# Feed-forward stages: the down product two rows behind the up product, deeper buffers between them, and weight splits on GpSimd tied to finished chunks

## What is computed

```python
x = x + 0.5 * L0_ffn(layernorm(x))      # stage ffn0a
x = x + L0_attn(layernorm(x))
x = x + 0.5 * L0_ffn(layernorm(x))      # stage ffn0b
x = x + 0.5 * L1_ffn(layernorm(x))      # stage ffn1a
x = x + L1_attn(layernorm(x))
x = x + 0.5 * L1_ffn(layernorm(x))      # stage ffn1b

def L0_ffn(x):   # "gated": hidden size 768, integer weights, scale 1/127
    h = silu(x @ wg.T) * (x @ wu.T)
    return h @ wd.T
def L1_ffn(x):   # not gated: hidden size 1024, float weights
    h = gelu(x @ w1 + b1)
    return h @ w2 + b2
```

## Time and profile before

| | us |
|---|---|
| median of 3 runs (2221.59 to 2228.74) | 2226.15 |
| the profiled execution | 2221.8 |
| its span | 2218.8 |
| TensorE busy | 2038.5 (92%) |
| VectorE busy | 1635.1 (74%) |
| ScalarE busy | 1360.3 (61%) |
| GpSimd busy | 512.7 (23%) |
| ffn0a, ffn0b, ffn1a, ffn1b: stretches of the span | 34 to 192, 1007 to 1178, 1178 to 1381, 2022 to 2218.8 |

### The profile page before, as it was taken

One profiled execution on the slowest core, in us unless ns is written; L12 is line 12 of the kernel. 1 busy time (PEld: TensorE's weight loads), 2 busy tenths in 40 slices (PEclk: granted clock), 3 DMA queues, 4 the chain that ended last, 5 costly groups with the idle time before them and its releaser, 6 DMA issues. The chain is left out here.

```text
span 2218.8 us, 44693 instructions
## 1 busy us (share of the span) xinstructions
PE 2038.5 (92%) x16837; PEld 1258.3 (57%) x16837; DVE 1635.1 (74%) x2894; ACT 1360.3 (61%) x2620; POOL 512.7 (23%) x570
## 2 busy tenths in 40 slices
PE   3998889999999999987998999959999999989998
PEld 2887733333333333355877888834444444448887
DVE  6776699999999999847774445868888888817333
ACT  3444348888888888833444544716777777753444
POOL 2100142211231231242003111973221212112110
PEclk9999979999999999998998999968999999989999
DMA  4002843253363363131001000785454655320000
GB/s 143 1 0 95 315 68 55 50 78 71 71 101 66 74 98 66 38 91 41 0 0 62 1 0 1 195 252 83 77 100 83 110 99 104 71 57 20 29 19 29
DMA packets 124377, 161.68 MB, mean 73 GB/s; under 512 B 54669, under 2 KB 77901, under 8 KB 124181
## 3 DMA queue, kind: packets, MB, share of 16 engines
q1 hardware_dynamic: 107108, 119.67, 25.9%
q0 software_dynamic: 16256, 37.82, 6.5%
q10 hardware_dynamic: 816, 1.57, 0.2%
HBM read 94.02 MB, written 63.70 MB: 71 GB/s over the span
## 5 line engine op out<-in xcount | busy, mean ns | idle before, releaser
L1523 ACT ACTIVATE att_probs<-att_s_exp 128x512 f32<-128x512 f32 (+3 forms) x1792 | 888.2, 552 | 222.1 <-PE att_s_exp L1422 98.9
L1555 DVE TENSOR_REDUCE att_maxes<-att_s_max 128x2 f32<-128x1024 f32 x640 | 773.6, 1223 | 69.9 <-PE att_s_max L1383 65.5
L1446 PE MATMUL att_o_ps<-att_probs,att_v_st 128*32 128x256 f32 (+1 forms) x6912 | 527.2, 377 | 19.5 <-ACT att_o_sb L1502 18.8
L1446 PEld LDWEIGHTS att_o_ps<-att_probs,att_v_st 128*32 128x32 f32 x6912 | 138.1, 108 | 268.3 <-issue 165.4
L1549 DVE CUSTOM_DVE_ANT_0 att_s_max<-att_s_max,mask_q 128x384 f32<-128x384 f32 (+3 forms) x512 | 237.2, 521 | 28.1 <-PE att_s_max L1383 24.8
L1383 PE MATMUL att_s_max<-first_k,first_q 62*128 62x512 f32 (+3 forms) x672 | 153.4, 444 | 41.3 <-DVE att_neg_max L1534 24.0
L1422 PE MATMUL att_s_exp<-first_q,first_k 64*128 64x512 f32 (+3 forms) x672 | 175.4, 476 | 2.6 <-ACT att_probs L1523 1.8
L1422 PE MATMUL att_s_exp<-w_lo,w_hi 64*128 64x512 f32 x640 | 164.7, 498 | 1.4 <-DMA w_lo<-att_m_parts 1.4
L1422 PEld LDWEIGHTS att_s_exp<-first_q,first_k 64*128 64x128 f32 x672 | 74.4, 186 | 132.0 <-ACT att_probs L1523 113.1
L1618 POOL TENSOR_TENSOR att_m_parts<-att_m_turned,att_zeros 32x128 fp32r<-32x128 f32 x64 | 29.0, 453 | 500.9 <-ACT att_m_turned L1489 368.8
L1422 PEld LDWEIGHTS att_s_exp<-w_lo,w_hi 64*128 64x128 f32 x640 | 63.1, 183 | 134.1 <-ACT att_probs L1523 123.5
(11 more groups left out here) (324 smaller groups left out, 4411.2 us busy)
## 6 DMA issues: line engine op xcount, KB each, us to landing
attention_rows<-att_o_sb POOLq DMA_DIRECT2D x64, 256.0 KB, 4.3
output_wide<-attention_weights POOLq DMA_DIRECT2D x36, 256.0 KB, 5.4
first_q<-q_parts SPq DMA_DIRECT2D x132, 64.0 KB, 5.5
first_k<-k_parts SPq DMA_DIRECT2D x66, 128.0 KB, 4.7
q_parts<-qkv_parts SPq DMA_DIRECT2D x16, 512.0 KB, 4.8
k_parts<-qkv_parts SPq DMA_DIRECT2D x16, 512.0 KB, 4.5
v_rows<-qkv_vt SPq DMA_DIRECT2D x16, 512.0 KB, 4.5
att_v_raw<-v_rows SPq DMA_DIRECT2D x32, 256.0 KB, 6.1
```

Source lines behind the costliest of these rows:

```text
L1446: mm = pe.matmul(o_ps[j * VW:(j + 1) * VW, cols], v_st[:, it.par, kt, j, :], probs[:, step % 2, j, cols], start=kt == 0 and part == 0, sto ...
L1523: act.activation(probs[:, step % 2, j, q0:512], s_exp[:, plan.bank[place], q0:512], ACT.Exp, scale=1.0 if causal else 0.25).then_inc(s["ex ...
L1555: v.tensor_reduce(maxes[:, qc, :, pairs, qt - 4 * qc, kc], banks, AX.X, ALU.max).then_inc(s["max_done"], 1)
```

## The change

1. TensorE runs down(f - 2) after up(f) (`BEHIND = 2`). The last two down products of a chunk come after up(0) and up(1) of the next, and at the end of a stage two are left to do after the last up product.
2. `h_hi` and `h_lo` have three buffers (gated) or four (not gated). In ffn0b `h_hi` lies in the tile `first_k`. `h`, `gate_act`, `up_ps` and `acc` stay as they are.
3. VectorE's `finish` moves from row 0 to row 1 and `measure` from row 1 to row 2.
4. GpSimd's split of each weight matrix in ffn0b is cut in two pieces of 128x1024. In both gated stages every pass but the first waits until x_new has counted further by two, that is for one more finished chunk: `hi` of piece m for 4m, `lo` of piece m for 4m + 2. The passes of ffn1a keep no such wait.

```diff
+BEHIND = 2
...
         h = sb("h", [P, 2, CHUNK], F32)
-        h_parts = [sb(f"h_{n}", [P, 2, CHUNK], F32R) for n in ("hi", "lo")]
+        HBUFS = 3 if gated else 4
+        assert F % HBUFS == 0
+        h_parts = [hi_tile[:, 0:HBUFS * CHUNK].rearrange("p (b n) -> p b n", n=CHUNK) if hi_tile else sb("h_hi", [P, HBUFS, CHUNK], F32R),
+                   sb("h_lo", [P, HBUFS, CHUNK], F32R)]
...
                     for f in range(F):
                         up(c, par, f, first)
-                        if f > 0:
-                            down(c, f - 1, first)
+                        if f >= BEHIND:
+                            down(c, f - BEHIND, first)
                         elif not first:
-                            down(c - 1, F - 1, False)
+                            down(c - 1, F + f - BEHIND, False)
                         if f == 2 and (follow or not last):
                             turn(pe, E, T, c + 1, 1 - par, s)
...
-                down(CHUNKS - 1, F - 1, False)
+                for f in range(F - BEHIND, F):
+                    down(CHUNKS - 1, f, False)
...
-                    if not first or f >= 2:
-                        act.wait_ge(s["down_done"], c * F + f - 1)
-                    act.activation(h_parts[0][:, f % 2, :], h[:, f % 2, :], ACT.Copy).then_inc(s["h_hi"], 1)
+                    if not first or f >= HBUFS:
+                        act.wait_ge(s["down_done"], c * F + f - HBUFS + 1)
+                    act.activation(h_parts[0][:, f % HBUFS, :], h[:, f % 2, :], ACT.Copy).then_inc(s["h_hi"], 1)
...
+                pieces = 2 if halve is not None else 1
                 for i in range(len(late.jobs)):
                     p.wait_ge(late.landed[i], 16)
...
-                    late.hi(p, i).then_inc(s["late_hi"], 1)
-                    p.wait_ge(s["late_hi"], i + 1)
-                    late.lo(p, i).then_inc(s["late_lo"], 1)
-                    p.wait_ge(s["late_lo"], i + 1)
+                    for n in range(pieces):
+                        rows, m = late.jobs[i][2] // pieces, i * pieces + n
+                        at = slice(n * rows, (n + 1) * rows)
+                        if gated and m:
+                            p.wait_ge(s["x_new"], 4 * m)
+                        late.hi(p, i, at).then_inc(s["late_hi"], 1)
+                        p.wait_ge(s["late_hi"], m + 1)
+                        if gated:
+                            p.wait_ge(s["x_new"], 4 * m + 2)
+                        late.lo(p, i, at).then_inc(s["late_lo"], 1)
+                        p.wait_ge(s["late_lo"], m + 1)
...
-                    if f == 0 and not first:
+                    if f == BEHIND - 1 and not first:
                         finish(c - 1, 1 - par, (0,))
...
-                    if f == 0 and not first:
+                    if f == BEHIND - 1 and not first:
                         finish(c - 1, 1 - par, (1,))
-                    if f == 1 and not first:
+                    if f == BEHIND and not first:
                         measure(c - 1)
```

More of the change, by code:

```diff
@@ L299, in load, with hi @@
         sp.dma_start(self.raw[i][:, :, :], src.rearrange("(k p) n -> p k n", p=P)).then_inc(self.landed[i], 16)
-    def hi(self, eng, i):
-        return eng.tensor_copy(self.jobs[i][0][0][:, :, :], self.value[i][:, :, :])
+    def hi(self, eng, i, at=slice(None)):
+        return eng.tensor_copy(self.jobs[i][0][0][:, at, :], self.value[i][:, at, :])
     def load_all(self, sp):
@@ L390, in _, with ffn_stage @@
             p.partition_all_reduce(peak_all[:, :], peak[:, :], P, bass.bass_isa.ReduceOp.max).then_inc(s["peak_all"], 1)
-def ffn_stage(nc, E, name, gated, out_dram=None, late=None, follow=False, issue=False, xt_first=None, xt_next=None, halve=None):
+def ffn_stage(nc, E, name, gated, out_dram=None, late=None, follow=False, issue=False, xt_first=None, xt_next=None, halve=None, hi_tile=None):
     F = (HID0 if gated else HID1) // P
@@ L443, in down @@
                             pe.wait_ge(s["x_new"], c * 2 - 1 + t // 2)
-                        mm = three_pass(pe, acc[:, t, :], pair(h_parts, slice(None), f % 2, slice(t * P, (t + 1) * P)),
+                        mm = three_pass(pe, acc[:, t, :], pair(h_parts, slice(None), f % HBUFS, slice(t * P, (t + 1) * P)),
                                         pair(E.w_down, slice(None), f, slice(None)), f == 0 and t % 2 == 0, f == F - 1,
@@ L573, in body @@
                                                in1=gate_act[:, f % 2, :], op0=ALU.mult, op1=ALU.mult).then_inc(s["h_ready"], 1)
-                    if f == 0 and not first:
+                    if f == BEHIND - 1 and not first:
                         finish(c - 1, 1 - par, (0,))
                     v.wait_ge(s["h_hi"], c * F + f + 1)
-                    if not first or f >= 2:
-                        v.wait_ge(s["down_done"], c * F + f - 1)
-                    v.tensor_tensor(h_parts[1][:, f % 2, :], h[:, f % 2, :], h_parts[0][:, f % 2, :].bitcast(F32),
+                    if not first or f >= HBUFS:
+                        v.wait_ge(s["down_done"], c * F + f - HBUFS + 1)
+                    v.tensor_tensor(h_parts[1][:, f % HBUFS, :], h[:, f % 2, :], h_parts[0][:, f % HBUFS, :].bitcast(F32),
                                     ALU.subtract).then_inc(s["h_lo"], 1)
-                    if f == 0 and not first:
+                    if f == BEHIND - 1 and not first:
                         finish(c - 1, 1 - par, (1,))
-                    if f == 1 and not first:
+                    if f == BEHIND and not first:
                         measure(c - 1)
@@ L1840, in program @@
                               raw=[raw[0].rearrange("p (k n) -> p k n", k=KD), raw[1].rearrange("p (k n) -> p k n", n=D)])
-                ffn_stage(nc, E, "ffn0b", True, late=ahead, follow=True, issue=True, xt_next=xt_next, halve=row)
+                ffn_stage(nc, E, "ffn0b", True, late=ahead, follow=True, issue=True, xt_next=xt_next, halve=row,
+                          hi_tile=E.first_k)
             outputs.close()
```

## The result

The changed kernel takes 2196.74 us (median of 4 runs, 2196.06 to 2197.41), the kernel before beside it 2223.87 (2218.39 to 2228.74). The ratio is 0.9879, with a 95% interval of 0.9853 to 0.9904: 27 us or 1.2% faster. Forecast were 2205 us in a range of 2195 to 2215.

What follows compares the result with a forecast made beforehand. TensorE, busiest in every stage, bounds the kernel; at most 51.7 us of idle and half-clock time could be won. Terms sum to 19.9 us off the 2226.15 us median, giving 2206; forecast 2205, range 2195 to 2215.

Steps and rivals of the forecast that it cites:

- The hole in ffn0b: Second chunk of ffn0b: TensorE's 10.65 us wait behind a stretched `normalise` goes and the clock recovers; +12.1 us.
- The hole in ffn1a: ffn1a: `normalise` still takes about 4 us, but TensorE's wait of 2.13 us and its clock fall go; +3.6 us.
- The recorded chain: ffn1a: h_lo of row 0 is ready 6.9 us after the last up product; TensorE asks after 8.4.
- The first chunk of the gated stages: ffn0a and ffn0b: nothing won, since up(5) waits about 1.9 us for h instead; -0.6 us for both.
- this walk: Instruction-by-instruction trace of the gated stages' start: second chunk's up(3) starts 0.7 us earlier, one 0.95 us down product less done.
- the reading that VectorE has a quarter of its time free: All four stages: VectorE, next busiest after TensorE, has a quarter or more of its time free.
- The ends of the stages: Last down product's wait of 1.20 (gated) or 0.90 us shrinks to 0.3 or none; +3.6 us over four stages.
- The last chunk of ffn0a: End of ffn0a: 0.86 us of waiting for h_lo goes, the `xn` wait and half clock stay; +1.0 us.
- Of ffn0b, -2.2: Last chunk of ffn0b: GpSimd's eighth pass and halving hold up VectorE; TensorE waits 5.5 us instead of 3.3; -2.2 us.
- the case that only `normalise` is held: Last chunk of ffn0b: GpSimd delays `normalise` alone, `xn` is there at 12.8 us; term -1.1 us.
- The boundaries between chunks: Ungated stages: 0.36 us lost at each instead of 0.46; with half of other waits, first chunk's above all, +2.4 us.

Runs made afterwards that it cites:

- h_lo later: Changed kernel, but in the gated stages VectorE makes h_lo of a row after h of the next row; 2182.7 us, ratio 0.9825.
- the rows alone: Changed kernel with GpSimd's splits as in the kernel before, so only two rows of distance and deeper buffers; 2202.2 us, ratio 0.989.
- the splits alone: Kernel before with only the new GpSimd passes (half pieces in ffn0b, tied to finished chunks); 2214.5 us, ratio 0.9948.
- the corner: Changed kernel with h_lo a row later in all stages, earlier lo passes, and last chunk's variance and root moved forward; 2175.7 us, ratio 0.9785.
- the repeat: Changed kernel run again without an edit, on the chip of the last experiments; 2191.9 us, ratio 0.9871.
- earlier splits: Changed kernel with each later lo pass waiting for the same count as its hi pass (4m, not 4m + 2); 2192.3 us, ratio 0.9855.

## Why the prediction came out as it did

**The hole in ffn0b, +12.1: right.** `normalise` takes 1.38 us, there is no wait above 1.6 us in the first chunks, and the clock stays at 1.00 there. From the stage's first up matmul to the second turn it takes 29.3 us instead of 42.1; less the down product that now comes later, 11.8 us are gained, against 12.1 less 0.3 for the first chunk. The two experiments with one part each show that this is the splits' doing: with them alone the hole is gone, without them it stays whole.

**The hole in ffn1a, +3.6: right.** `normalise` still takes 4.11 us there, and TensorE waits for nothing around it. (The recorded chain, 0.7 + 0.6 + 0.7 + 4.1 + 0.6, adds up to 6.7 us and not 6.9; against 8.4 that changes nothing.)

**The first chunk of the gated stages, nothing: right,** and in the places given. The changed kernel in ffn0a:

```profile
50.58 0.50 PE L133 MATMUL ffn0a_up<-front0a_xt_lo,w_gate_hi 128*128 128x512 f32 x1 [1.61 <-DVE ffn0a_h L585]
```

This is up(5), for which 50.4 and a wait of 1.9 us were forecast. The first and the second half of `finish` let down(0) go at 63.12 and 64.52, where I had 62.8 and 64.3. What I did not draw from this walk is that VectorE's chain with its waits for ScalarE is nearly as long as TensorE's work in every gated chunk: of 17.7 us VectorE works 12.9 and waits 3.8 for ScalarE in the middle of ffn0a, and 13.8 and 3.7 in ffn0b. So the reading that VectorE has a quarter of its time free is right as a busy share and wrong as slack, which is 0.2 to 1 us a chunk. (It is the second busiest engine in the gated stages alone; in the others ScalarE is, by the same rows.) The run with h_lo later shows what that slack is worth, about 2.5 us in ffn0a.

**The ends of the stages, +3.6: right.** The last down product of ffn0a waits 0.38 us (forecast 0.3), that of ffn1b not at all.

**The last chunk of ffn0a, +1.0: right** in kind: 1.95 us of waiting for `xn` and 0.16 for `finish` instead of 3.26 in two pieces, and half clock after it, as before. **Of ffn0b, -2.2: the mechanism right, the size too large.** The wait is 3.9 us where I said 5.5, so that 0.7 us more are waited than before and not 2.2. Counted from up(0) at 1134.96, the pass ran from 8.3 to 10.7 as forecast, `xn` was ready at 12.8 and not at 13.9, and TensorE asked for it at 9.0 and not at 8.4. The pass stretched the product of 128x8 from 0.17 to 2.05 us, as assumed from the stretched h_lo; but the halving, for which I had counted 0.6 us (it took 0.87), held nothing up. In part that is luck in the timing: the next product with two inputs began 0.03 us before it, and `normalise` only 0.17 us before its end, so that the run doesn't show what a halving would hold. That `xn` at 12.8 is also what I gave for the case that only `normalise` is held is a coincidence; the 2.05 us rule that case out. The Trainium skill's rule (SBUF — State Buffer, Who interferes with whom), that two SBUF inputs put a VectorE instruction in line for the shared port pair, agrees with the 2.05 us.

**The boundaries between chunks, +2.4: this is the term that was mis-sized,** and it makes the largest part of the difference, about 6.6 of 9.1 us; 1.5 more are the last chunk of ffn0b. I had taken one of them, 0.46 us against 0.36, for the ungated stages and counted nothing in the gated ones. The turns of two chunks that follow each other, before and after, in ffn1b and in ffn0b:

```profile
2103.41 1.03 PE L242 MATMUL ffn1b_T<-ident,front1b_xn 128*128 128x128 f32 x8
...
2127.04 1.04 PE L242 MATMUL ffn1b_T<-ident,front1b_xn 128*128 128x128 f32 x8
```

```profile
2057.02 1.04 PE L243 MATMUL ffn1b_T<-ident,front1b_xn 128*128 128x128 f32 x8
...
2080.36 1.04 PE L243 MATMUL ffn1b_T<-ident,front1b_xn 128*128 128x128 f32 x8
```

```profile
1067.66 1.03 PE L242 MATMUL ffn0b_T<-ident,front0b_xn 128*128 128x128 f32 x8
...
1085.81 1.04 PE L242 MATMUL ffn0b_T<-ident,front0b_xn 128*128 128x128 f32 x8
```

```profile
1072.49 1.03 PE L243 MATMUL ffn0b_T<-ident,front0b_xn 128*128 128x128 f32 x8
...
1090.22 1.04 PE L243 MATMUL ffn0b_T<-ident,front0b_xn 128*128 128x128 f32 x8
```

A chunk takes 23.34 us instead of 23.63 in ffn1b and 17.73 instead of 18.15 in ffn0b. Over the five middle distances the mean saving is 0.31 and 0.34, and 0.34 in ffn0a and 0.29 in ffn1a: 6.4 us over the four stages in these alone. Seven boundaries in each at about 0.32 would be 9 us, against 2.4 in the forecast, which had the first waits of ffn1a and ffn1b in it as well. The run with the rows alone has this saving and the run with the splits alone doesn't (23.34 and 23.65 us in ffn1b), so that it comes from the distance and the place of `finish`. Two things were wrong. In the gated stages I read the list of waits, which leaves out gaps of 0.13 to 0.28 us, since a matmul is shown as busy for longer than until the next can start (0.39 us where the next up matmul starts after 0.23); start times show them. And where not gated I took the time from the start of a release to TensorE's start from h_lo (2121.84 to 2122.76 in the kernel before, 0.92 us), while after `finish` it is 0.74:

```profile
2055.47 0.68 DVE L563 SCALAR_TENSOR_TENSOR x<-ffn1b_acc,ffn1b_xb 128x512 f32 x1
...
2056.21 0.39 PE L133 MATMUL ffn1b_acc<-w_lo,ffn1b_h_hi 128*128 128x256 f32 x1
```

So this matmul starts 0.31 us after the one before it, where 0.12 is usual, and 0.19 us are lost there and not 0.36. Counted from the whole chunk, a boundary in ffn1b lost 0.61 us before the change and loses 0.32 after it, against the 23.02 us that the run with the corner shows.

**The sum.** By stage the forecast was 1.6 + 10.5 + 5.7 + 2.1 = 19.9 us and the profiled executions show 3.3 + 13.4 + 7.7 + 4.6 = 29.0. The median moved by 27; in the profiled pair the attentions took 4.8 us more. The mechanisms named in the forecast are those that the runs show, but that the median lies in the range at 2196.7, near its lower end of 2195, is partly luck: the sum was 9 us short, and the repeat gave 2191.9, a gain of 28.9.

## What to carry to other kernels

An engine that works strictly in order and waits in the middle of each step for another engine has a chain longer than its busy time: here 16.7 to 17.5 us of 17.7, at a busy share of 73 to 78% of such a chunk. Add the waits to the work before calling the rest slack, and put the instruction that waits behind the next step's first one; that (with the halves of `finish` moved together behind it) was worth about 2.5 us in a stage and made a helper's passes free. More distance between producer and consumer hides only what lies between them: it hid a late h_lo of 4 us and none of a late h. And short losses at a boundary that comes 28 times are read from start times, from one chunk to the next, since a list of waits leaves them out.

## What the runs showed that was not expected

The clock after the same wait is not the same. In the last chunk of ffn0a TensorE waited 2.0 us for `xn` both in the changed kernel and in the run with earlier splits. The window from 170 to 180 us, first of the changed kernel, then of that run:

```profile
170.00:180.00 10.00, 7.89 (x39) 6.59 (x38) 6.90 (x19) 5.25 (x9) 0.00 (x0) 0.83 0.00 0
```

```profile
170.00:180.00 10.00, 7.89 (x47) 6.60 (x46) 8.11 (x21) 6.66 (x11) 0.00 (x0) 1.00 0.00 0
```

The granted clock was 0.83 in one and 1.00 in the other, with 39 and 47 matmuls in the same 10 us, and from the turn to the last down matmul it took 13.3 and 11.7 us (ffn0a as a whole 152.9 and 151.9, since the second opened more slowly). The repeat of the changed kernel fell to 0.83 again after the same 1.95 us. A wait of about 2 us can thus cost another 1.5 us or nothing, and it did so in two kernels with the same code at this place; what decides it these runs don't show. It is part of what separates two executions, and a stage length compared between runs must be freed of it first.
